# State-space scan: four states of 32 channels on the partitions instead of 128 channels of one state

## The reference

```
xr = x @ W_in.T + b_in;  xc, res = split(xr)
u  = silu(conv3(xc))                        # 256 channels
dlt, B, C = split(u @ W_x.T)                # 64 + 16 + 16
delta = softplus(dlt @ W_dt.T + b_dt)       # 256 channels
state[d, n] = exp(delta[d] * A[d, n]) * state[d, n] + delta[d] * u[d] * B[n]
y[d] = sum over n of state[d, n] * C[n]
out = (y * silu(res)) @ W_out.T + b_out
```

## Time and profile before

| | |
|---|---|
| median of 3 runs | 1052.18 us (1051.52 to 1057.14) |
| profiled execution | 1056.04 us |
| its span, first to last instruction | 1054.3 us |
| mean granted clock of TensorE | 0.937 |
| moved by DMA | 151.8 MB, mean 144 GB/s |

### The profile page before, as it was taken

The page is one execution under the profiler, slowest core; times in us unless marked ns, Lnnn a source line. Parts: engine busy times, 40 slices in busy tenths (PEclk is TensorE's granted clock), DMA queues, the critical chain, the costliest instruction groups (busy, mean ns, idle before and its releaser), DMA issues.

```text
span 1054.3 us, 11228 instructions
## 1 busy us (share of the span) xinstructions
PE 911.8 (86%) x3358; PEld 431.3 (41%) x3358; DVE 768.3 (73%) x1717; ACT 655.8 (62%) x1030; POOL 516.0 (49%) x412
## 2 busy tenths in 40 slices
PE   6557877888889888999999999999999889978975
PEld 5334334343444344445354444435443343333432
DVE  3222514988599769995999688978998989799821
ACT  4435558568757866677778765897687437634221
POOL 2112135555647464645565555666475545555311
PEclk9668898999899989999999999999999898998976
DMA  3000106523553446336337545545354717665320
GB/s 144 10 0 25 67 0 217 196 100 124 197 190 111 137 175 227 116 130 213 136 122 233 186 154 171 190 168 198 128 185 171 236 47 254 222 190 184 107 90 11
DMA packets 49325, 151.83 MB, mean 144 GB/s; under 512 B 4976, under 2 KB 13296, under 8 KB 49264
## 3 DMA queue, kind: packets, MB, share of 16 engines
q1 hardware_dynamic: 49264, 151.12, 41.9%
HBM read 148.21 MB, written 2.88 MB: 143 GB/s over the span
## 4 chain that ended last, share of the span: by engine, by line
PE 47%; DVE 26%; ACT 12%; issue 6%; POOL 5%; DMA 2%; SPq 0%; DVEq 0%; POOLq 0%; ACTq 0%
PE yp L1484 10%; DVE dA L983 10%; PE mp L1428 4%; PE mp L1443 4%; PE fp L1249 4%; PE pp L1363 4%; PE pp L1229 3%; PE fp L1265 3%; ACT L117 3%; DVE hs L990 3%; DVE he L941 2%; PE mp L1229 2%; PE pp L1333 2%; ACT dA L1208 2%; PE mp L1452 2%
## 5 line engine op out<-in xcount | busy, mean ns | idle before, releaser
L710 POOL TENSOR_TENSOR dbu<-du,b_row 128x1024 f32<-128x1024 f32 x128 | 301.5, 2359 | 169.7 <-DVE dA L983 151.0
L983 DVE TENSOR_TENSOR_SCAN dA<-dA,dbu 128x512 f32<-128x512 f32 x256 | 312.4, 1220 | 67.5 <-POOL dbu L710 34.9
L1484 PE MATMUL yp<-hs,ident 128*128 128x512 f32 x512 | 268.4, 628 | 14.1 <-DVE hs L990 13.9
L1208 ACT ACTIVATE dA<-delta,pr 128x512 f32<-128x512 f32 x256 | 173.6, 685 | 80.5 <-DVE hs L990 76.3
L990 DVE TENSOR_TENSOR hs<-dA,c_row 128x512 f32<-128x512 f32 x256 | 176.9, 691 | 9.8 <-PE yp L1484 1.1
L117 ACT ACT_TABLE_LOAD x130 | 166.8, 1283 | 2.4
L1484 PEld LDWEIGHTS yp<-hs,ident 128*128 128x128 f32 x512 | 89.2, 195 | 142.6 <-issue 84.8
L1428 PE MATMUL mp<-cont,ex_ 64*128 64x512 f32 x128 | 79.1, 701 | 12.7 <-DVE he L941 11.4
L1265 PE MATMUL fp<-w,hT 128*128 128x129 f32 x512 | 68.6, 285 | 13.7 <-ACT hT L1044 7.0
L1432 PE MATMUL mp<-cont,ex_ 64*128 64x512 f32 x128 | 79.3, 703 | 0.1
L1265 PEld LDWEIGHTS fp<-w,hT 128*128 128x128 f32 x512 | 64.2, 197 | 36.4 <-ACT hT L1044 14.9
(11 more groups left out here) (216 smaller groups left out, 1353.8 us busy)
## 6 DMA issues: line engine op xcount, KB each, us to landing
b_row<-held SPq DMA_DIRECT2D x104, 512.0 KB, 4.9
c_row<-held SPq DMA_DIRECT2D x104, 512.0 KB, 4.3
gsp<-gheld SPq DMA_DIRECT2D x64, 512.0 KB, 6.2
xin<-L_attn_x SPq DMA_DIRECT2D x8, 256.0 KB, 4.7
out<-xb SPq DMA_DIRECT2D x8, 256.0 KB, 3.4
ex_<-c_ex SPq DMA_DIRECT2D x1, 1001.0 KB, 6.8
b_row<-c_ps SPq DMA_DIRECT2D x1, 768.0 KB, 8.2
pr<-c_pr SPq DMA_DIRECT2D x1, 567.0 KB, 9.1
```

The source lines that it names most:

```text
L710: pool.tensor_tensor(out=dbu[:, j % 2, :].rearrange("p (r t) -> p r t", r=2), in0=d, in1=b_n, op=ALU.mult).then_inc(dbu_r.sem, 1)
L983: dve.tensor_tensor_scan(out=dA[:, half], data0=dA[:, half], data1=dbu[:, j % 2, half], initial=0.0, op0=ALU.mult, op1=ALU.add).then_inc(h ...
L1208: act.activation(out=dA[:, r * SEQ:(r + 1) * SEQ], in_=delta[:, i % 2, c, :], func=ACT.Exp, scale=mA[:, c, 2 * k + r:2 * k + r + 1]).then_ ...
L1484: pe.matmul(yp[:, :], lhsT=ident[:, :], rhs=hs[:, j % 2, r * SEQ:(r + 1) * SEQ], start=(s % PAIRS == 0 and r == 0), stop=(s % PAIRS == PAI ...
```

## The change

The partitions of the scan now hold four blocks of 32 channels; each block works on another four of the 16 states. A batch still has 16 steps, each of two 512-token halves: half c of the channels, own state k (0 to 3) of the block, and a pair j of channel groups.

- delta and delta u, made half by half (128 channels each), are written to memory and loaded back, four groups of 32 channels behind one another and each repeated for the four blocks (`d4`, `u4`). `delta` and `du` have one buffer instead of two.
- B and C are loaded once per batch in two parts of 1 MiB (`bc4`): each partition gets the four states of its block. The class `Rows` and its slots go.
- The host turns the columns of A and W_x so that each block finds its own states first.
- A step's two sums go to two strips of 32 columns of the array, by a 128 x 32 matrix of ones at equal channels (`stack`). They are one unit of PE's thread, and it waits for both halves.
- Transfers for the spread are a new thread U on SP. All order strings are new (ACT's is shown).

```diff
 ORDER = {
...
     "ACT":
-        "FPFFFFFFFFFFFFFFFFFFFFFFFFPFFPFPFFPFFPFPPPFFFFFEEEFFFFEFFFFPFPPPPFPFPFPFFPFSFFSPSFPSPSPSSPSPPSSSFSFS"
-        "FFSSSFEEESFSFSFFEFFSFFPSFSSPSSPSPSSPSPSFPSSFPPFFSPFFSPSFFSPSFPSSPPPSFSFSSFFSSFSSEEESFSSFFFEFFSFFSSPS"
-        "FSPSSPSSPFPSSSPSPSFPPFFSPFPFSPSPSSSPFFPFSPSPSPSPPSPFSSFPFFPFSSSEFESEFSSFFEFFSFFSPFSSPSSPSSPSSPPSSPFS"
-        "PFPFFSSPFPEFFEPFEPSFSPSPPSPPPPSSFPSFPSFFFPSSEESESSEFSSSFFFEFFSFFSSFPSPSSPSPSSPSSPSSPFSPFPFFFFPSPFSFE"
-        "PSPFESESSPPPSPPPEPSFSPSFFPSFFPSSSSEEESFSSFFFEFFSFFSFSPSPSSSPSSPSPSPSSPFSPFPFFSPSFPSPSEFPSPSEESFPFFPS"
-        "PPSPSPESPFSFPFFPFSSESSEESFFSFFEFFSFSFSPFPSSSPSSPSPSSPSPSSPPSPESPESEPSSSPSPSPPESPSPSPSPSPSPPSEEESSSES"
-        "SSPSSSPSSPSSPSPSSPSPPPSPSESPESPSPSPESSPESSPSSSSSSSPSSPSSPSSPPSPSPSSSESSEESSEPPEPPEPPPEEEEEE",
+        "FPFFFFFFFFFFFFFFFFFFFFFFFFPFPFFPPFFFPFPFPPFFFFFEEEFFFFEFFFFPFPPPPFPFPFFPFPFFPFPPFSPSSPSPPFSSFSSFFSFS"
+        "SSSEEESFSFFEFFSFPFFPSSPFPPSPSSPSPFPSFSPSFSPFPFSPFSPSFFPSFPSSSSFSFSFFSSFSESEESFFSESSFFSPFPFSFFSSPSSPF"
+        "PSPSSPPFPSFSPFFPSSPFPFSPFFPSSFPPSPSPPSSPFSPFFFPFSSFESFSEESFFSSFFEFFSFSPSPSSPSPFPSPSSPFSPFPSSFPSPSFPS"
+        "SPFSSPFSFSEPFEEPPSSPPSPEPFSFPSFFPFSSFESFSEESFFSSFEFSFFSPFSPSSPSSPSPSPSSPPFPFSSPSPSPFPFSPFFSPFFESSFPE"
+        "PESPSPSPPEPSFSFFSFPSFSSSEESEFSSFFSESFSFPFSPFFSSPSSFPSPSPSSPFPSFSPSESPSEFPESPSFPFSPFPFSFSEPFSSPSPSPPF"
+        "PSFFFPFSSPSSEEFESSFSFFSEFFSFPSSPFSSPFSSPPSSPSSPPSPSSPSPSPSEPSSPSEEPSPPPSSPSEPSPSSPPSSSESESSESSSESSSP"
+        "SPSSPSSPSPSSPSPSPSSPSEPESEPSSSPPSPSESPPSSSSPSPSSPSPSPSSPSSSPSSSSSSSSSSESESEEPPEPEEPPPEPEEEE",
...
-STEP_ORDER = [(0, k) for k in range(PAIRS)] + [(1, k) for k in reversed(range(PAIRS))]
+STEP_ORDER = [(c, k, j) for c in range(IC) for k in range(OWN) for j in range(PER // 2)]
...
-        b_row = sb("b_row", [P, B_SLOTS, 2 * SEQ])
-        c_row = sb("c_row", [P, C_SLOTS, 2 * SEQ])
+        d4 = sb("d4", [P, GROUPS, SEQ])
+        u4 = sb("u4", [P, GROUPS, SEQ])
+        bc4 = sb("bc4", [P, 2, 2, 2, SEQ])
+        stack = sb("stack", [P, LANES])
...
-        delta = sb("delta", [P, 2, IC, SEQ])
-        du = sb("du", [P, 2, IC, SEQ])
+        delta = sb("delta", [P, IC, SEQ])
+        du = sb("du", [P, IC, SEQ])
...
-        held = nc.dram_tensor("held", (2, 2, STATES, SEQ), F32, kind="Internal").ap()
+        held = nc.dram_tensor("held", (2, 2, BLOCKS, 4 * SEQ), F32, kind="Internal").ap()
+        dheld = nc.dram_tensor("dheld", (2, IC, LANES, PER, SEQ), F32, kind="Internal").ap()
+        uheld = nc.dram_tensor("uheld", (2, IC, LANES, PER, SEQ), F32, kind="Internal").ap()
...
+                    for h in range(2):
+                        yield True
+                        if h == 0:
+                            sp.wait_ge(bc_out.sem, bc_out.at(i, 16))
+                        if i >= 1:
+                            sp.wait_ge(dbu_r.sem, dbu_r.at(i - 1, last_of_half(h)))
+                            sp.wait_ge(hc_r.sem, hc_r.at(i - 1, 2 * last_of_half(h)))
+                        src = held[i % 2, h, :, :].rearrange("s (a t) -> s a t", a=1)
+                        sp.dma_start(bc4[:, h, :, :, :].rearrange("p w k t -> p (w k t)"),
+                                     src.broadcast_to([BLOCKS, LANES, 4 * SEQ])).then_inc(bc_in[h].sem, 16)
+
+            def deltas():
+                for i in range(BATCH):
+                    for c in range(IC):
+                        lanes = lambda a: a[i % 2, c, :, :, :].rearrange("r g t -> g r t")
+                        groups = lambda a: a[i % 2, c, :, :, :].rearrange("(a r) g t -> a r (g t)", a=1
+                                                                         ).broadcast_to([BLOCKS, LANES, PER * SEQ])
+                        own = slice(c * PER, (c + 1) * PER)
+                        yield True
+                        sp.wait_ge(du_r.sem, du_r.at(i, c + 1))
+                        if i >= 2:
+                            sp.wait_ge(u_in[c].sem, u_in[c].at(i - 2, 16))
+                        sp.dma_start(lanes(uheld), du[:, c, :]).then_inc(u_out[c].sem, 16)
+                        yield True
+                        sp.wait_ge(start_r.sem, start_r.at(i, c + 1))
...
+                        sp.dma_start(lanes(dheld), delta[:, c, :]).then_inc(d_out[c].sem, 16)
+                        yield True
+                        sp.wait_ge(u_out[c].sem, u_out[c].at(i, 16))
+                        if i >= 1:
+                            sp.wait_ge(dbu_r.sem, dbu_r.at(i - 1, (c + 1) * C_STEPS))
+                        sp.dma_start(u4[:, own, :].rearrange("p g t -> p (g t)"), groups(uheld)
+                                     ).then_inc(u_in[c].sem, 16)
+                        yield True
...
+                            sp.wait_ge(dA_r.sem, dA_r.at(i - 1, 2 * (c + 1) * C_STEPS))
+                        sp.dma_start(d4[:, own, :].rearrange("p g t -> p (g t)"), groups(dheld)
+                                     ).then_inc(d_in[c].sem, 16)
...
-                pool.tensor_tensor(out=du[:, b, :, :], in0=delta[:, b, :, :], in1=du[:, b, :, :],
-                                   op=ALU.mult).then_inc(du_r.sem, 1)
...
+                for c in range(IC):
+                    yield True
+                    pool.wait_ge(del_r.sem, del_r.at(i, c + 1))
+                    pool.wait_ge(mx_ps.sem, mx_ps.at(i, 1))
+                    pool.tensor_tensor(out=du[:, c, :], in0=delta[:, c, :], in1=du[:, c, :],
+                                       op=ALU.mult).then_inc(du_r.sem, 1)
...
+                        b_n = bc4[:, k // 2, 0, k % 2, :].rearrange("p (a t) -> p a t", a=1)
+                        pool.tensor_tensor(out=dbu[:, n % 2, :].rearrange("p (r t) -> p r t", r=2),
+                                           in0=u4[:, c * PER + 2 * j:c * PER + 2 * j + 2, :],
+                                           in1=b_n.broadcast_to([P, 2, SEQ]), op=ALU.mult).then_inc(dbu_r.sem, 1)
...
+                                if n >= 2:
+                                    dve.wait_ge(sum_ps.sem, 2 * (n - 1))
+                            dve.tensor_tensor(out=hs[:, n % 2, half], in0=dA[:, half],
+                                              in1=bc4[:, k // 2, 1, k % 2, :], op=ALU.mult).then_inc(hc_r.sem, 1)
...
+                        if i >= 1:
+                            act.wait_ge(u_out[c].sem, u_out[c].at(i - 1, 16))
+                        act.activation(out=du[:, c, :], in_=pp[:, :], func=ACT.Silu,
...
+                            if s % C_STEPS == 0 and r == 0:
+                                act.wait_ge(d_in[c].sem, d_in[c].at(i, 16))
...
+                            act.activation(out=dA[:, r * SEQ:(r + 1) * SEQ], in_=d4[:, g, :], func=ACT.Exp,
+                                           scale=mA[:, IC + g, k:k + 1]).then_inc(dA_r.sem, 1)
...
-                            pe.matmul(yp[:, :], lhsT=ident[:, :], rhs=hs[:, j % 2, r * SEQ:(r + 1) * SEQ],
-                                      start=(s % PAIRS == 0 and r == 0), stop=(s % PAIRS == PAIRS - 1 and r == 1)
+                        pe.wait_ge(hc_r.sem, 2 * (n + 1))
+                        if s % C_STEPS == 0 and n:
+                            pe.wait_ge(yg_r.sem, i * IC + c)
                         for r in range(2):
+                            g = 2 * j + r
+                            pe.matmul(yp[LANES * g:LANES * (g + 1), :], lhsT=stack[:, :],
+                                      rhs=hs[:, n % 2, r * SEQ:(r + 1) * SEQ], start=(k == 0), stop=(k == OWN - 1)
                                       ).then_inc(sum_ps.sem, 1)
```

More of the change, by code:

```diff
@@ L48 @@
+        "PSPPSSSPEFESEPSPFFSSFSFSFSEEEPSSSSFPSSPSPPSSPSPSEESESSSSSSPEEESPSPSSSSSPSPPSSPSEEESSSPSSSSSSSSSSPEEE"
+        "PPEEEEEE",
     "DVE":
[L49 to L52, removed]
@@ L118, in need, with last_of_half @@
             self.loaded = sets[0]
-PAIRS = STATES // 2
-STEPS = IC * PAIRS
-B_SLOTS, C_SLOTS = 3, 3
-STEP_ORDER = [(0, k) for k in range(PAIRS)] + [(1, k) for k in reversed(range(PAIRS))]
-class Rows:
-    def __init__(self, slots):
-        self.slots, self.slot, self.load, self.after = slots, {}, {}, {}
-        free_after, loads = [-1] * slots, [0] * slots
-        for j in range(BATCH * STEPS):
-            i, s = divmod(j, STEPS)
-            twin = i * STEPS + 2 * PAIRS - 1 - s
-            if PAIRS <= s < PAIRS + slots:
-                self.slot[j], self.load[j] = self.slot[twin], self.load[twin]
-                continue
-            at = min(range(slots), key=lambda x: free_after[x])
-            loads[at] += 1
-            self.slot[j], self.load[j], self.after[j] = at, loads[at], free_after[at]
-            free_after[at] = twin if PAIRS - slots <= s < PAIRS else j
-    def loads_before(self, at, j_end):
-        return sum(self.slot[j] == at for j in self.after if j < j_end)
-B_ROWS, C_ROWS = Rows(B_SLOTS), Rows(C_SLOTS)
+BLOCKS = 4
+OWN = STATES // BLOCKS
+LANES = P // BLOCKS
+GROUPS = INNER // LANES
+PER = GROUPS // IC
+STEPS = IC * OWN * PER // 2
+C_STEPS = STEPS // IC
```

(12 more changed lines are left out.)

194 lines of the change are left out of this document (85 added, 109 removed).

## The result

The change made the kernel slower by a third: 1414.9 us (median of 4 runs, 1412.1 to 1426.3) against 1052.2, a ratio of 1.345 (95% interval 1.337 to 1.354). The profiled execution took 1416.0 us around a span of 1414.3. The forecast was 1023, its range ended at 1075, and faster had a chance of 0.64.

The account below looks back on a forecast made before the run. PE was taken to bound the middle (96% busy), DVE the later scans. Sums gain 44 us, the spread loses 15, net 29: 1052 - 29 = 1023 us; the forecast case's range 1004 to 1046, overall 988 to 1075.

Parts of the forecast that it names:

- the spread: Step sizes and products through memory and back: 10 us lost at first scan, 0 between, 5 at last; 15 in all.
- the rival beside it: New loads and writes run on four of 16 DMA engines, 100 us per batch: about 1080 us, chance 0.19.
- under B and C: Loading B and C as two 1 MiB transfers per batch: gain 0 to 3 us, taken as 0.
- an expected 0.97: PE's granted clock in the middle, some 9 us of PE work; DVE then leads, so taken as 0.
- The new order: All five queues reordered: 157 table loads for 130, 35 us of ACT, 7 us at a fifth.
- the 0.93: Busiest engine's share assumed from 478 to 811 us, as three nearly even queues cannot keep 96%: 311 us, gain 22.
- The sums: A step's two scan sums on PE: 1.1 us instead of 1.72, 79 us of PE over 128 steps.
- The gain of 44 us by stages: Time gained from cheaper sums across the scan stages: 8, 10, 22 and 4 us, tail 0.
- the one in which DVE paces: PE and ACT give way and DVE runs at 96%, 302 us in the middle: 986 us, chance 0.13.
- The spread that is not covered: Each of six scans between starts 4.5 us late, 27 us lost: 1051 us, chance 0.12.
- the wrong case: Signs: DVE or POOL idle until new loads, 1 MiB over 10 us, late gate rows, middle clock near 0.9.
- the right case: Signs: paired sums starting together, PE below 295 us in three middle batches, 157 table loads, DVE leading there.

## Why the prediction was wrong

**The step that failed** is the spread, "10 for the first scan, 0 between, 5 for the last". It took 3.4 us for a write and 6.8 us for a load from rows of transfers whose outermost dimension is 128, while the rival beside it said that the new ones would run on four engines. That was so. In the run as made the write and the load of the first step sizes alone take 27.9 and 24.1 us of the chain:

```profile
167.65 27.90 DMA dheld<-delta
...
195.57 24.12 DMA d<-dheld
```

and the first scan starts 47 us later than before, not 10. With the transfers on 16 engines the same term measures 14.9 us (187.9 against 173.0), the upper end that was written down, of which 2.9 are a delta that the new order of ACT brings later (ready at 166.3 us against 163.3). The batches behind the first lose 15 more, where 0 and 5 stood.

**The rival's price failed too.** Its condition held, its chance of 0.19 was too low for a condition that a stated rule decides, and its 1080 us was off by 335. It added up what four engines carry, 100 us per batch, and took that as hidden when it fits beside the other work. The rate was sound: the run as made has 100.84 MB in 21.6% of 16 engines over 1414.3 us, 20.6 GB/s per engine where 21.4 was taken, and by it the same sum gives some 103 us per batch (an estimate from those rows). What failed is the hiding. Even at an order made for it the kernel comes to 1143.9; that this is within 6% of the price is luck, for beside 1020.8 on 16 engines it is 123 us, where the price put 28. In the order of the change little was hidden. Each half needs a write, its landing and a load, one after the other; three transfers share the four engines in the rows from SP's timeline; and SP waits for each landing with the gate rows queued behind. "On SP the next gate rows are queued behind these waits" was in the text, under B and C, with no price; it became the largest wait for a transfer, 189.9 us. The clock fell with it, from an expected 0.97 to 0.82.

**The new order** was priced by its table loads alone, 7 us inside the 0.93. The count was right and the price too high (29 loads fewer gave 1 us on 16 engines). Nor did ACT grow where the loads were put: it has 249 us of work in scans 3 to 5, as before, and not 277. The rest of the order, which got no price, cost what is left: 77 us lie between two orders of one and the same kernel on 16 engines (1097.6 and 1020.8), 49 more than the same search gave the kernel before (28).

**The sums held.** A pair takes 0.98 us by its start distance where 1.1 was taken. The gain of 44 us by stages is 31 when the pairs are taken away from the good order and 38 in the other, and in scans 3 to 5 PE on 16 engines has 273.8 us of work, under the mark of 295 (296.7 as made, at the lower clock). The Trainium skill's drain at a change of mode (TensorEngine Tiling, Key Properties) was to make it 1.30 with the neighbours' loss; 31 to 38 us of time are below the 54 that this left for busy PE, but so they would be at 1.1, and no run here took the drain by itself.

**Of the rivals**, the one in which DVE paces is what the kernel on 16 engines does in its better order, in the middle. Its 986 us were not reached, since the first scans, the start and the end do not follow; and its 302 us for the middle are PE's 290 at 96%, while DVE's 281 would have given 292. The spread that is not covered, 27 us between the scans, measured 15 on 16 engines.

The signs that the text named for the wrong case all came: scans released by the new loads, those loads landing after well over 10 us, gate rows late, a clock well below 0.97. Of those for the right case, the pairs and the 157 loads came in the run as made; DVE leading in the middle did not.

## What to carry to other kernels

Before pricing a transfer, look at its outermost dimension: a broadcast or a regrouping that puts a small count there leaves most DMA engines idle, and splitting it into transfers that each begin with 32 partitions brought back 317 us here. A rival that turns on how transfers are served is priced twice, by what they carry and by the chain of write, landing and load with all that is queued behind the waits. And where queues follow a written order, a change of the work is compared at orders made for either: 363 us slower as it came, this one, with its transfers split, is level with the old kernel, and either is 3% faster, once both are planned anew.

## What the runs showed of the hardware

- What a DMA engine carries depends less on how many others work than on the form of the transfer. In the windows above two engines move 52 GB/s and four 78 to 100 (61 to 108 over the run as made, at a share of 0.25): 20 to 26 GB/s each. At all 16 the kernel before moves 339 GB/s, 21 each, in loads to 128 partitions, and the kernel with split transfers 232, 14.5 each, most of it in loads to 32 partitions:

```profile
300.00:306.00 6.00, 5.72 (x14) 2.18 (x14) 5.28 (x7) 5.70 (x7) 1.12 (x1) 1.00 1.02 339
```

  Why the split loads are slower per engine stays open, and so does how much of what the spread still costs in that kernel is theirs; no run has the spread in another form over 16 engines.
- Transfers over all 16 engines are held when four of these are taken. The gate rows land in 5.9 us in the median, as before (6.2), but their longest took 36.3 us, where it was 10.1 before and is 15.9 with all transfers split.
- Splitting has its own price at the queue: in SP's timeline four transfers take 1.7 to 1.9 us to issue where one took 0.5. With two writes and two loads per half of the channels that is some 5 us of SP for each half, and part of the 15 us ahead of the first scan.
